# A routed adapter and feed-forward kernel: each element's output stores are issued in the next element, behind its first adapter fetch

## The reference

```python
y = jnp.einsum('bsi,boi->bso', x, weight[adapter_ids])         # stage 1
base_out = jnp.einsum('btd,od->bto', y, base_W) + base_b       # stage 2
probs = softmax(y @ router_W.T + router_b)                     # 15 router outputs
w = top-8 of probs, summed by expert_map                       # gates of 8 experts
h = jnp.einsum('btd,erd->bter', y, A)
lora = jnp.einsum('bter,eor->bto', h * w[..., None], B) * 2.0
out = x + base_out + lora
```

## Time and profile before

| | |
|---|---|
| median of 3 runs | 414.61 us |
| lowest, highest | 413.88, 416.39 us |
| the profiled execution | 415.91 us, with a span of 414.1 us from its first to its last instruction |
| mean granted TensorE clock | 0.995 of full speed |
| TensorE matmuls busy | 403.5 us, 97% |
| VectorE busy | 296.4 us, 72% |
| ScalarE busy | 155.2 us, 37% |
| DMA | 64.73 MB, 156 GB/s over the span |

### The profile page before, as it was taken

How to read it: one execution, slowest core, us unless ns; L and a number is a source line. 1 busy time by engine, 2 the same in 40 slices (tenths; PEclk the granted TensorE clock), 3 DMA queues, 4 the chain that set the end, 5 groups by cost and what they waited for, 6 DMA issues and landing times.

```text
span 414.1 us, 6381 instructions
## 1 busy us (share of the span) xinstructions
PE 403.5 (97%) x2272; PEld 374.1 (90%) x2272; DVE 296.4 (72%) x577; ACT 155.2 (37%) x238; POOL 0.8 (0%) x8
## 2 busy tenths in 40 slices
PE   8999999799899999999999999999999999999997
PEld 7788998599898999889998899988999899988996
DVE  2477999689848886499746987388854997558643
ACT  3358173563116620364305622166302652045200
POOL 0000000000000000000000000000000000000000
PEclk9999999899999999999999999999999999999999
DMA  6989602573035820568015750257304680145002
GB/s 193 366 299 370 254 0 109 197 285 122 0 125 195 311 80 0 199 223 285 2 51 203 287 169 0 101 203 295 110 0 162 228 289 30 51 169 187 1 2 101
DMA packets 25598, 64.73 MB, mean 156 GB/s; under 512 B 2546, under 2 KB 11634, under 8 KB 25586
## 3 DMA queue, kind: packets, MB, share of 16 engines
q1 hardware_dynamic: 25586, 64.57, 43.7%
HBM read 56.18 MB, written 8.39 MB: 156 GB/s over the span
## 4 chain that ended last, share of the span: by engine, by line
PE 78%; DVE 6%; DMA 6%; SPq 5%; issue 2%; ACT 2%
PE y_ps L732 25%; PE y_ps L734 12%; PE pl_ps L755 5%; PE pl_ps L757 5%; PE pl_ps L756 5%; PE x_ps L767 4%; PE x_ps L769 4%; PE x_ps L768 4%; DMA x_raw<-in_xT 4%; DMA w_raw<-in_wT 3%; PE z_ps L767 2%; PE z_ps L768 2%; PE z_ps L769 2%; DVE w_lo L458 1%; PE w_ps L767 1%
## 5 line engine op out<-in xcount | busy, mean ns | idle before, releaser
L732 PE MATMUL y_ps<-x_split,w_hi 128*128 128x512 f32 x496 | 174.7, 397 | 3.2 <-DVE y_sum L470 2.9
L734 PE MATMUL y_ps<-x_split,w_lo 128*128 128x256 f32 x496 | 138.4, 279 | 0.0
L732 PEld LDWEIGHTS y_ps<-x_split,w_hi 128*128 128x128 f32 x496 | 93.7, 189 | 26.0 <-DVE w_lo L458 3.2
L734 PEld LDWEIGHTS y_ps<-x_split,w_lo 128*128 128x128 f32 x496 | 93.9, 189 | 0.0
L458 DVE TENSOR_TENSOR w_lo<-w_raw,w_hi 128x1024 fp32r<-128x1024 f32 x62 | 75.7, 1224 | 18.9 <-ACT w_hi L357 16.4
L357 ACT CAST w_hi<-w_raw 128x1024 fp32r<-128x1024 f32 x62 | 64.9, 1050 | 16.0 <-DMA w_raw<-in_wT 15.6
L349 ACT COPY y_sum<-y_ps 128x256 f32<-128x256 f32 x62 | 23.0, 371 | 117.4 <-PE y_ps L734 117.4
L755 PE MATMUL pl_ps<-pl_hi,y_hi 128*128 128x432 f32 x128 | 46.0, 360 | 0.7 <-DVE pl_lo L604 0.6
L756 PE MATMUL pl_ps<-pl_lo,y_hi 128*128 128x432 f32 x128 | 45.8, 358 | 0.0
L757 PE MATMUL pl_ps<-pl_hi,y_lo 128*128 128x432 f32 x128 | 45.8, 358 | 0.0
L470 DVE TENSOR_TENSOR y_sum<-y_ps,y_sum 128x256 f32<-128x256 f32 x62 | 26.1, 421 | 26.8 <-ACT y_sum L349 26.2
(11 more groups left out here) (136 smaller groups left out, 608.0 us busy)
## 6 DMA issues: line engine op xcount, KB each, us to landing
w_raw<-in_wT SPq DMA_DIRECT2D x63, 512.0 KB, 3.3
res<-in_x SPq DMA_DIRECT2D x16, 512.0 KB, 4.5
out<-res SPq DMA_DIRECT2D x15, 512.0 KB, 2.6
x_raw<-in_xT SPq DMA_DIRECT2D x14, 512.0 KB, 6.0
hi_raw<-in_base_t SPq DMA_DIRECT2D x4, 368.0 KB, 5.9
st_raw<-in_base_t SPq DMA_DIRECT2D x4, 368.0 KB, 6.7
pl_raw<-in_base_t SPq DMA_DIRECT2D x2, 576.0 KB, 7.1
x_raw<-in_xT SPq DMA_DIRECT2D x4, 256.0 KB, 3.9
```

The source lines that it names most:

```text
L732: nc.tensor.matmul(y_ps[:, c % 2, :], w_hi[:, s, k, :], x_split[:, k, :, :].rearrange("p s t -> p (s t)"), start=(k == 0), stop=False)
L734: mm = nc.tensor.matmul(y_ps[:, c % 2, 0:T], w_lo[:, s, k, :], x_split[:, k, 0, :], start=False, stop=(k == KC - 1))
```

## The change

Each element's two stores leave the end of the element's list and are issued in the next element, right behind the fetch that its first chunk frees. The last element's stores stay where they are. For that, `element` gets a function `store_previous`, which it calls at c = 0. Element 1 is taken out of the loop, since it stores element 0 with the waits that element 0 has (`store_first`), and the loop covers 2 to 6.

```diff
+            def store_first():
+                sp.wait_ge(pl_added, 1)
+                store(0, 0, slice(0, D))
+                sp.wait_ge(v_added, 1)
+                store(0, 1, slice(0, D))
+
-            def element(b, last=False):
+            def element(b, store_previous, last=False):
                 this = adapter(b)
                 nxt = None if last else adapter(b + 1)
                 for c in range(OC):
                     if c + W_SLOTS < OC or not last:
                         sp.wait_ge(y_ps_done, OC * b + c + 1)
                         load_w(this if c + W_SLOTS < OC else nxt, (c + W_SLOTS) % OC)
+                    if c == 0:
+                        store_previous()
                     if c in (4, 5):
                         load_res(b, c - 4)
                 if not last:
                     load_x(b + 1)
-                store_element(b, last)
...
             load_x(1, first=True)
-            sp.wait_ge(pl_added, 1)
-            store(0, 0, slice(0, D))
-            sp.wait_ge(v_added, 1)
-            store(0, 1, slice(0, D))
-
-            with sp.Fori(1, NB - 1) as b:
-                element(b)
-            element(NB - 1, last=True)
+
+            element(1, store_first)
+            with sp.Fori(2, NB - 1) as b:
+                element(b, lambda: store_element(b - 1))
+            element(NB - 1, lambda: store_element(NB - 2), last=True)
+            store_element(NB - 1, last=True)
```

## The result

The changed kernel is slower: 417.94 us median of 9 runs (417.07 to 419.60) against 414.96 us of the kernel before (9 runs, 412.71 to 417.14). The ratio is 1.0086, with a 95% interval of 1.0059 to 1.0114. The profiled execution took 417.20 us with a span of 415.4 us.

What follows compares the result with a forecast made beforehand. TensorE, busy for 97% of the span, was taken as the bound, so gains had to come from its stops and slow clock: 3.06 + 1.83 = 4.89 us off 415.20 gave 410.3 us, range 408.5 to 413.2.

Steps and rivals of the forecast that it cites:

- the cause of the 3 us stop: Element 1, stage 1: only SP's queue order, a store ahead of chunk 4's fetch, delayed that fetch by 4.67 us.
- Terms one and two: Element 1: the stop before chunk 4, 3.06 us, and the slow clock after it, 1.83 us; sum 4.89 us.
- The clock term: Four chunks behind element 1's stop ran at mean clock 0.87, costing 1.83 us, which was to go with the stop.
- rival B: Clock would have dropped in few ordinary runs, so only the 3.06 us stop is gained: 412.1 us, chance 0.10.
- (1): Element 1: chunk 4's fetch ahead of element 0's stores arrives in time; residual stall 0, at most 0.5 us.
- (3): Chunk 5's fetch behind 1 MB of stores, elements 2 to 7: 0.5 to 1.1 us late, cost 0.
- (2): Elements 2 to 7: stores go behind chunk 4's fetch; `res` is needed 11 us later, so nothing waits for them.
- the time of the group: At 402 GB/s the fourth transfer is home 3.9 us after the first; the worst row made it 1.8 us late.
- the price of lateness: Chunk 5's fetch, elements 2 to 7: up to 1.2 us late is free; 1.8 us late costs 0.6 us each.
- Rival A: Stores return partly as late fetches, 1.8 us late in elements 2 to 7, losing 3.6 us: 413.9 us, chance 0.15.
- Rival D: Slower through chunk 5's fetch behind stores, elements 2 to 7; gain gone at 2.0 us late: 419.3 us, chance 0.06.
- The rule of ring order: Skill's rule: DMA engines take a queue's descriptors in ring order, so a fetch doesn't start before stores ahead of it.

Runs made afterwards that it cites:

- run 2: Changed kernel with its two stores parted, one behind each of the first two fetches in every element: 417.82 us, ratio 1.0076.
- run 3: Only element 1 has the new order; from element 1 on the stores stand at their element's end as in the kernel before: 412.40 us, ratio 0.9916.
- run 4: Kernel before with all stores but the last element's issued from GpSimd's queue, each when its adds are done: 412.01 us, ratio 0.9907.
- run 6: Changed kernel with both stores one fetch later, behind chunk 5's fetch and ahead of chunk 6's: 415.37 us, ratio 1.0013.
- run 7: Changed kernel with stores of elements 0 to 6 cut to 256 of 1024 columns, same places and waits: 411.48 us, ratio 0.9912.
- Run 8: As run 3, but element 0's stores stand behind element 1's second fetch (chunk 5) instead of its first: 411.29 us, ratio 0.9922.
- run 9: Stores at the changed kernel's times but issued from GpSimd's queue, SyncE having only fetches and loads: 421.41 us, ratio 1.0166.
- run 1: The kernel before once more, no edit, to see each execution's mean clock: 415.23 us, ratio 0.9996.
- run 5: Kernel before with both residual loads moved up behind the fetch that chunk 1 frees, stores left at the end: 419.54 us, ratio 1.0104.
- run 10: Changed kernel with element 0's stores left in front of element 1's fetches; elements 2 to 7 as changed: 420.72 us, ratio 1.0140.

## Why the prediction was wrong

- **What bounds the kernel, and the cause of the 3 us stop:** right. SP's order held the fetch. In every kernel that freed it (the change, runs 2 to 4 and 6 to 9) the stop went, while it stayed in runs 1, 5 and 10, which didn't.
- **Terms one and two, 4.89 us:** right in size. Run 8 has 55.27 - 50.87 = 4.40 us of it. The clock term is there in most executions (at most in 40 of 53 and in 11 of 12, run 1), so rival B, which had it in few, was wrong. The runs of the kernel before at a clock of 1.000 beside runs 1 to 4 had a median of 413.7 us (6 runs), those below it one of 415.6 us (18 runs).
- **(1), residual stall 0, at most 0.5 us in element 1:** mis-sized. The change left two stops and element 1 gained 3.45 us. The account there looked at chunk 4 and VectorE's backlog. Chunk 4 was indeed in time. The chain of the changed kernel says that the stops came from chunk 5's fetch, which was costed in (3) for elements 2 to 7 only, and element 1 has the same two stores ahead of it (5.3 us to landing):

```profile
68.65 5.26 DMA w_raw<-in_wT
...
73.93 1.06 ACT w_hi L362
...
75.02 1.22 DVE w_lo L463
76.24 0.35 DVE y_sum L475
```

- **(2), moving the stores costs `res` nothing:** right; no residual load waited for a store.
- **(3), chunk 5's fetch 0.5 to 1.1 us late, cost 0:** this is the step that failed. The fetch was 1.73 us late and each element lost 0.94 us on the mean. Two terms of the step were too small, the time of the group of transfers and the price of lateness.
- **The time of the group:** the choice was the 402 GB/s of the earlier trace rows over the burst of the earlier trace rows. By it the fetch of chunk 5 was to be home 3.3 + 3.9 = 7.2 us after the issue of the fetch of chunk 4. The burst gave 7.9 us, and 7.78 us is what it took, so the late bound of 1.8 us was the true one. The burst is of loads alone, and so is run 5, with 7.91 us; it wasn't the mix of stores and loads that made the low choice wrong. The reason given for it was that the stores' data can move while chunk 4 is still landing. They did, but at the cost of chunk 4, which landed in 4.09 us instead of 3.3; the other three transfers then needed 3.69 us more, close to the 3.9 expected. With loads in the stores' place (run 5) the first landed in 3.25 us and the others needed 4.66 us more. The windows of the changed kernel show the first microseconds (us; busy shares; then clock, DMA share and GB/s):

```profile
168.00:169.00 1.00, 1.00 (x8) 0.87 (x7) 0.88 (x1) 0.09 (x1) 0.00 (x0) 1.00 1.01 246
169.00:170.00 1.00, 1.00 (x8) 0.87 (x7) 0.40 (x2) 0.37 (x1) 0.00 (x0) 1.00 0.83 201
170.00:171.00 1.00, 1.00 (x8) 0.87 (x7) 0.97 (x4) 0.59 (x1) 0.00 (x0) 1.00 1.01 414
171.00:172.00 1.00, 1.00 (x7) 0.88 (x6) 0.79 (x2) 0.99 (x2) 0.00 (x0) 1.00 1.03 422
```

  Those of run 5, as far behind the issue of its fetch:

```profile
173.30:174.30 1.00, 1.00 (x8) 0.87 (x7) 0.87 (x3) 1.00 (x2) 0.00 (x0) 1.00 0.89 299
174.30:175.30 1.00, 1.00 (x8) 0.87 (x7) 0.91 (x2) 0.95 (x3) 0.00 (x0) 1.00 1.04 410
```

  In the first two microseconds 447 KB moved with stores, and 709 KB with loads.
- **The price of lateness:** 1.2 us free and then one for one gave 0.53 us for 1.73 us late. Element 3 lost 0.86 us. The stretch that the prediction took for stage 1 begins at 167.79, but TensorE began element 3 at 167.59, and it entered chunk 6 at 184.23, not 184.43:

```profile
167.59 0.40 PE L732 MATMUL y_ps<-x_split,w_hi 128*128 128x512 f32 x1
...
184.23 0.40 PE L732 MATMUL y_ps<-x_split,w_hi 128*128 128x512 f32 x1
```

  So the slack was 1.0 us and not 1.2. The stop in the changed kernel bears this out. The last pair before it starts at 180.09, the next should at 180.44 and starts at 181.18, 0.74 us late, and 1.73 - 0.74 = 0.99. The first pair behind the stop takes 181.61 - 181.18 = 0.43 us from start to start instead of 0.35, and with these 0.08 us the loss is 0.82 us of the 0.86:

```profile
180.09 0.39 PE L737 MATMUL y_ps<-x_split,w_hi 128*128 128x512 f32 x1
180.32 0.27 PE L739 MATMUL y_ps<-x_split,w_lo 128*128 128x256 f32 x1
...
181.49 0.28 PE L739 MATMUL y_ps<-x_split,w_lo 128*128 128x256 f32 x1
181.61 0.40 PE L737 MATMUL y_ps<-x_split,w_hi 128*128 128x512 f32 x1
```

  The 0.58 us of idle time in its row is less than the 0.74, since it is counted from the modelled end of the matmul before. The same restart stands in my clock term, where the first pair takes 0.43 us too (77.93 to 78.36).
- **Rival A** had the mechanism and the place, with 413.9 us. Three terms make the distance to 417.94: 0.94 instead of 0.6 us in six elements (2.0 us), the residue of element 1 (4.89 - 3.45 = 1.4 us), and the clock term, which the kernel before doesn't pay in every run (an estimate of 0.4 us: 14 of these 53 + 12 executions were at a clock of 1.000, times 1.83). That gives 417.7 us, about the time measured. **Rival D** had its sign and its threshold of 2.0 us late; the threshold was computed with 0.2 us too much slack, without the restart and without element 1, and so the kernel went over it at 1.73.
- **The rule of ring order** that spoke against the change pointed at the right fetch. Run 9 shows that the order in the queue isn't needed for the delay: off the queue, the same stores delay the fetch as much.
- **What stays open:** why a store slows the fetch in front of it while a load of the same size doesn't (runs 5 and 6), and why the group takes nearly the same time either way. Whether it is the direction in HBM, the reading of SBUF or something in the DMA engines was not tried.

## What to carry to other kernels

A transfer that goes out in a gap of the DMA engines should stay there: the stores of element 2 took 2.6 and 2.7 us to land in the kernel before, and 4.9 and 5.3 us in their new place. Before it is moved, look up when the data would then flow, and not only when it is issued or when it is needed. Where a wait at one place blocks a queue, reorder at that place alone (here element 1, worth 0.8%) and leave the loop as it is. If the bound of an unmeasured burst lies between two rows, and both ends differ in the answer, take the row of a whole burst of as many transfers over the rate of a stretch from inside one: here four transfers of 512 KB took 7.7 to 8.5 us from the first issue to the last landing in four kernels, whatever their direction. And take the start of a stage from the row of its first instruction, since 0.2 us of slack was 0.2 us in each of six elements.

## What the runs showed of the hardware

- A 512 KB store issued 0.6 us behind a 512 KB fetch made that fetch land in 3.8 to 4.1 us instead of 3.1 to 3.3 in elements 2 to 6 of the changed kernel; a load in the same place left it at 3.1 to 3.4 (the kernel before and run 5). With stores of 128 KB it still landed in 3.7 to 3.9 us (run 7). Exceptions are element 1 of run 3, with 3.4 us beside a store, and element 2 of run 9, with 3.5.
- Behind a fetch and 1 MB of other transfers, a fetch landed in 4.9 to 5.6 us behind stores (the changed kernel, run 6) and in 5.1 to 5.8 us behind loads (run 5).
- A fetch and two stores together moved 246 and 201 GB/s in their first two full microseconds, at a DMA share of 1.01 and 0.83; in the next five the rate was 406 to 426 GB/s at a share of 1.01 to 1.04.
- Stores from GpSimd's queue at the same time as fetches from SyncE's took 4.6 and 6.8 us to land in element 3 of run 9, and the fetch 5.7.
- The granted clock fell from 1.00 to 0.50 behind the 3 us stop in all four traces that have it (2.5 to 2.9 us of idle time; before, runs 1, 5 and 10). It also fell behind the stop in front of a stage 2 product of element 1 in runs 2 and 7, where that stop was 2.3 us; in the ten other traces that stop was 1.5 us and it didn't.
